# Leaving out TensorE's fifteen idle products of the identity at the start of a routed two-layer kernel

## The reference, cut to what matters

```
w   = weights[subjects]                       # 8 adapters of 32x32, one for each sample
z   = einsum('bct,bcd->bdt', x, w)            # tokens of a sample are mixed
logits = z @ Wg + bg                          # 4 experts
top 2 of 4, softmax, then for each expert the 1024 best tokens:
    out[sel] += gelu(tok @ W1[i]) @ W2[i] * p
x = x + out
gate, up, down with low-rank adapters by sample, silu(gate) * up, then a 256x256 product:
x = x + (h @ (w * scale).T + bias)
```

## Time and profile before

| | |
|---|---|
| median of three runs | 585.85 us (585.65 to 586.32) |
| profiled execution, its own time | 585.41 us |
| its span, first to last instruction | 583.6 us |
| PE busy | 567.9 us, 97% |
| PE on the chain that ended last | 93% |
| DVE on that chain | 5% |
| the idle products (line 1488) on that chain | 3.35 + 0.85 + 0.64 us |

### The profile page before, as it was taken

One profiled execution on the slowest core, in us unless ns is written; L12 is line 12 of the kernel. 1 busy time (PEld: TensorE's weight loads), 2 busy tenths in 40 slices (PEclk: granted clock), 3 DMA queues, 4 the chain that ended last, 5 costly groups with the idle time before them and its releaser, 6 DMA issues.

```text
span 583.6 us, 10462 instructions
## 1 busy us (share of the span) xinstructions
PE 567.9 (97%) x3629; PEld 475.9 (82%) x3629; DVE 371.4 (64%) x904; ACT 242.6 (42%) x548; POOL 138.6 (24%) x121
## 2 busy tenths in 40 slices
PE   7888999999999999999999999999999999999996
PEld 5766999999999999978878788788788788787885
DVE  7899667646775567675584474665655645755733
ACT  2664567748756655553312323224033223223110
POOL 2002311747346343664021030030030120100000
PEclk9999999999999999999999999999999999999999
DMA  8994677774285231434013032041041050220012
GB/s 326 343 361 177 200 244 222 196 182 72 47 259 145 47 41 20 128 62 136 1 46 102 8 109 47 0 133 22 0 137 16 4 140 9 76 49 4 13 25 37
DMA packets 64799, 61.06 MB, mean 105 GB/s; under 512 B 37456, under 2 KB 56656, under 8 KB 63472
## 3 DMA queue, kind: packets, MB, share of 16 engines
q1 hardware_dynamic: 53312, 37.97, 21.4%
q0 software_dynamic: 9264, 22.22, 15.6%
q10 hardware_dynamic: 2176, 0.26, 0.3%
HBM read 45.17 MB, written 19.47 MB: 111 GB/s over the span
## 4 chain that ended last, share of the span: by engine, by line
PE 93%; DVE 5%; DMA 1%; issue 0%; ACT 0%; POOL 0%; SPq 0%; DVEq 0%
PE bank L1455 26%; PE bank L1456 25%; PE bank L1457 25%; PE bank L1762 5%; PE bank L1720 3%; PE bank L1488 1%; PE bank L1471 1%; PE bank L1581 1%; DVE passed L887 1%; PE bank L1590 1%; PE bank L1712 1%; PE bank L1494 1%; PE bank L1729 1%; PE bank L1730 1%; PE bank L1539 1%; DVE passed_n L862 1%
## 5 line engine op out<-in xcount | busy, mean ns | idle before, releaser
L765 ACT ACTIVATE act<-bank 128x512 f32<-128x512 f32 x64 | 38.2, 598 | 182.9 <-PE bank L1762 182.9
L1411 DVE TENSOR_TENSOR prod<-bank,act 128x512 f32<-128x512 f32 x64 | 44.2, 691 | 97.5 <-PE bank L1762 97.1
L1267 DVE TENSOR_TENSOR hid_lo<-hf,hid_hi 128x512 fp32r<-128x512 f32 (+1 forms) x80 | 46.7, 585 | 52.5 <-ACT hf L686 52.1
L1455 PE MATMUL bank<-w_hi,hid_hi 128*128 128x256 f32 x256 | 71.7, 280 | 0.0
L1456 PE MATMUL bank<-w_lo,hid_hi 128*128 128x256 f32 x256 | 71.4, 279 | 0.0
L1457 PE MATMUL bank<-w_hi,hid_lo 128*128 128x256 f32 x256 | 71.3, 279 | 0.0
L683 ACT ACTIVATE hid_hi<-bank 128x512 fp32r<-128x512 f32 (+1 forms) x80 | 41.1, 514 | 65.0 <-PE bank L1457 63.3
L513 POOL DMA_INDIRECT x_rows<-y_sb,slot_row x32 | 52.6, 1644 | 43.1 <-ACT y_sb L653 27.3
L502 POOL DMA_INDIRECT xg<-flat_rows,slot_row x32 | 33.6, 1051 | 97.7 <-DVE slot_row L1112 49.3
L1455 PE MATMUL bank<-xs_hi,w_hi 128*128 128x512 f32 (+1 forms) x158 | 56.5, 357 | 0.0
L531 POOL DMA_INDIRECT b_pair<-b_rows,b_row x8 | 8.0, 1000 | 198.5 <-PE bank L1810 197.9
(11 more groups left out here) (326 smaller groups left out, 1269.8 us busy)
## 6 DMA issues: line engine op xcount, KB each, us to landing
w_raw<-in_L_ffn_W SPq DMA_DIRECT2D x8, 1024.0 KB, 6.9
flat_rows<-x_sb SPq DMA_DIRECT2D x8, 520.0 KB, 5.3
x_sb<-in_x SPq DMA_DIRECT2D x8, 512.0 KB, 8.6
x_rows<-in_x SPq DMA_DIRECT2D x4, 1024.0 KB, 8.1
outT<-out_sb SPq DMA_DIRECT2D x120, 32.0 KB
xT<-in_xT SPq DMA_DIRECT2D x3, 1024.0 KB, 7.4
xT<-in_xT SPq DMA_DIRECT2D x2, 512.0 KB, 10.6
wdT<-in_wdT SPq DMA_DIRECT2D x1, 1024.0 KB, 6.0
```

The lines of the kernel that those rows point to most:

```text
L765: act.activation(act1[h % 2][:, :], bank[h % 2][:, :], ACT.Silu).then_inc(silu1, 1)
L1267: dve.tensor_tensor(lo[:, n], hf[s % 2][:, n], hi[:, n].bitcast(f32), ALU.subtract).then_inc(hid0, 1)
L1411: dve.tensor_tensor(prod[par][h][:, :], bank[2 + h % 2][:, :], act1[h % 2][:, :], ALU.mult).then_inc(prod1, 1)
L1455: pe.matmul(out, lh, rh, start=start, stop=False, skip_group_check=True)
```

## The change

The function `idle_products` and its four calls are taken out. Nothing else is touched; the order on DVE and the DMA queue SP is the same, and on ACT and POOL only line numbers differ. Later lines of the kernel carry numbers that are lower by 5 (from `logits_of`), 8 (from the wait for `blocks_in`) and 9 (from the search).

```
-            def idle_products(n, into):
-
-                for _ in range(n):
-                    pe.matmul(into[:, 0:P], ident, ident, start=True, stop=True)
-
             def logits_of(half, adapters):
...
-            idle_products(7, bank[7])
             for i in range(7):
                 z_products(i)
                 if i in (2, 4, 6):
                     z_by_token(i // 2 - 1)
-                elif i in (1, 3):
-                    idle_products(2, bank[7])
             pe.wait_ge(blocks_in, 1)
...
             for n in range(ROWS_FIRST):
                 item(n)
-            idle_products(4, bank[4])
```

## The result

The changed kernel takes 587.86 us (median of 22 runs, 585.63 to 589.72), the kernel before in the same job 585.81 us (22 runs, 585.40 to 587.05). The ratio is 1.0026, 95% interval 1.0016 to 1.0035: a small loss, clear of no change; it stands just over the 0.2% that I had named, which lies inside its interval. (The ratio takes all runs into account and lies near that of the means, 1.0025; the medians' own is 1.0035.) The time lies in the predicted range (585.5 to 588.0), but not at 586.3, and the spread says more than the median: 8 of the changed kernel's runs lie between 585.6 and 587.2 us and 14 between 587.2 and 589.7. The mean granted clock of each of them parts them at the same place: 0.998 to 1.000 in the 8, 0.992 to 0.996 in the 14.

What follows compares the result with a forecast made beforehand. PE holds 93% of the chain and is full from 60 to 578 us, so the first 60 us set the end. Start +0.44 and search 0, added to the 585.85 us median, gave 586.3 us; range 585.5 to 588.0.

Steps and rivals of the forecast that it cites:

- no difference to be seen: Whole kernel: the forecast change lies below the 0.2% (1.2 us) that its times can tell; chance of same 0.66.
- a late rise (+0.44): Start: without idle products the clock rises at 13.33 us, so the turn at line 1482 starts at 14.72, not 14.28.
- rival 3: Search: the clock falls in the 1.5 us pause at 25.6 to 27.1 us; +1.5 us, 587.8 with part 1; chance 0.14.
- The path: PE's start delays line 908, then `slot_row`, POOL's gather and the end, one for one; gather at 54.5, not 54.1 us.
- rival 4: Start: the clock does not rise before the logits; +5 us, 591 us; chance 0.03.
- The data: Pieces of xT land at 6.98, 9.55, 12.17, 13.48 and 14.85 us; products start at about 7.03, 9.60 and 12.2 us.
- The rise: Start: PE's clock rises at 13.33 us, from first product at 7.03 plus 5.6 busy plus 0.70 pause; 12.6 to 14.5, chance 0.42.
- 5.6 us of PE busy: Start: PE busy time from its first product until the clock rises, taken from the one case in the trace.
- Rival 1: Start: the pause does not delay the rise, at 12.6 us or sooner; cost 0.0 to 0.15 us, 585.9 us; chance 0.18.
- rival 2: Start: the 0.70 us pause restarts the count, rise at 15.2 us; +1.18 us, 587.0, up to +1.7; chance 0.17.
- The four ahead of the search: Idle products behind the first 12 mixed rows: removal lengthens PE's pause to about 1.5 us, no clock fall, 0 us.

Runs made afterwards that it cites:

- e1: The changed kernel again, no edit; 589.84 us against 588.40 for the kernel before, ratio 1.0016.
- e4: Kernel before without the two pairs of idle products behind the calls on xT pieces 1 and 2; 588.79 us against 588.40, ratio 1.0003.
- e2: Kernel before without only the four idle products behind the first mixed rows; 588.13 us against 588.40, ratio 0.9996.
- e5: Kernel before plus five idle products at the search's end; 587.97 us against 588.11, ratio 1.0000.
- e10: Kernel before without the seven idle products ahead of the data, plus five at the search's end; 586.84 us against 585.93, ratio 1.0014.
- e9: Kernel before with one mixed row moved from the last search step to the one before it; 585.69 us against 585.93, ratio 1.0001.
- e11: Kernel before plus five idle products at the search's end and six products of zeros ahead of the identity wait; 586.23 us against 585.93, ratio 0.9999.
- e3: Kernel before without the eleven idle products of the start, last four kept; 589.82 us against 588.40, ratio 1.0023.
- e8: The changed kernel once more, in the job of e5 to e7; 590.57 us against 588.11 for the kernel before, ratio 1.0032.
- e12: The changed kernel a third time; 586.97 us against 586.38 for the kernel before, ratio 1.0018.
- e7: Kernel before without the eleven idle products of the start, four kept, five added at the search's end; 588.71 us against 588.11, ratio 1.0006.
- e6: Kernel before without all fifteen idle products, five added at the search's end; 588.74 us against 588.11, ratio 1.0009.

## Why the prediction was right or wrong

**The level and the direction.** The time lies in the range, but "no difference to be seen", the likeliest case, isn't what the runs show. The loss was to be the sum of a late rise (+0.44) and nothing; it is a late rise of 0 to 1.3 us and, in about half the runs, a fall of the clock on top. The forecast was +0.44 us, measured were +2.05 in median and +1.45 in mean; that this stayed in the range is owed to the upper end, which rival 3 had set with a fall at another place. The path was right: line 908 came 0.92 us later, the gather 0.88 us (54.96, forecast 54.5), and the last product of PE 0.98 us. In this profile the chain runs from `slot_row` over DVE's `w_lo` (line 1257) and not over the gather; both wait for `slot_row`. In rival 4 the sum compares the end of the turn (16.23 us) with the start of the one before (14.28); put right it is +4.6 us and not +5.

**The data (right, with a spread I left out).** Calls on pieces 1 and 2 started at 7.47 and 9.94 us in the changed kernel's first profile, for 7.03 and 9.60; in e1 they started at 6.99 and 9.46. The loads themselves vary by some 0.5 us, and without idle products in front PE follows them.

**The rise (right mechanism, size of the term off).** The profiles in a row give the rise and line 908's second addition:

| kernel | eleven at the start | clock up, us | line 908, us |
|---|---|---|---|
| before | in | 9.7 | 19.94 |
| e4 (seven of them) | in | 9.1 | 20.01 |
| e2 | in | 7.9 | 19.89 |
| e5 | in | 9.6 | 20.43 (data 0.50 late) |
| e10 (four of them) | in part | 10.9 | 20.41 |
| e9 | in | 8.5 | 20.24 (data 0.31 late) |
| e11 (and six of zeros) | in | 6.5 | 20.52 (piece 5 late) |
| e3 | out | 10.7 | 19.95 |
| e8 | out | 13.0 | 20.33 |
| e12 | out | 13.9 | 20.77 |
| changed | out | 13.9 | 20.86 (data 0.35 late) |
| e7 | out | 15.2 | 21.12 |
| e1 | out | 15.2 | 21.06 |
| e6 | out | 15.5 | 21.25 |

For the kernels without the eleven the working holds: I had 0 for a rise before 12.2 us (e3: +0.01), +0.44 for 13.33 (e8, 13.0: +0.39), +1.18 for 15.2 (e1 +1.12, e7 +1.18). What failed is the moment of the rise. The sum's 5.6 us of PE busy are the time from PE's first product at 4.04 us to the one rise on record, at about 9.65 us; that a pause adds to them was my estimate. No run shows 5.6 us as a fixed time: over these profiles the rise comes 3.5 to 8.4 us after PE's first product. It differs from run to run of one kernel, with 13.0, 13.9, 13.9 and 15.2 us in four profiles of the changed kernel. Rival 1 (e3, 10.7 us), the forecast (13.0 to 13.9) and rival 2 (15.2 to 15.5) all occur with the same program up to the logits. The start is then worth about 0.7 us, not 0.44: 0.74 in median (e7 against e5), and 0.66 as the difference of the mean of line 908 over the table's seven kernels with none of the eleven (20.76) and its five with at least seven of them and nothing added ahead (20.10).

**The four ahead of the search (right).** Cost 0: e2 0.9996, e6 equals e7. The pause of 1.45 us never showed a fall in a profile (changed, e1, e2, e6, e8, e12).

**Rival 3, the fall (right that there is one, wrong in place, and about right in price).** I had it behind the pause at 27 us, deciding the search, +1.5 us. It came at 49.3 us (e1) and 48.2 us (e3), where it hits the folds, +1.68 us there and 1.5 at the gather, and in e10 at 21.1 us. It lasted 3.4 us each time, and not 5.6 us of PE busy; PEclk is 1.00 in all fourteen profiles from 28 to 47 us, so none shows a slow step of the search as that rival had it. I had passed over the search's end although show its 0.75 us wait; I compared single waits and looked at the longest, and the clock had not fallen there in the one execution I had.

**How the median comes out.** In the jobs, 50 of 138 runs of the kernel before lie more than 1.2 us above their job's fastest. The mean granted clock says more than such a mark. It leaves out the time before the first rise (the changed kernel's profile, up at 13.9 us, has 0.999) and counts what is slow behind it: e1 and e3, with a fall, have 0.997. (So does e8's profile, whose only low stretch is the last 3.1 us, behind PE's last product; one run at 0.997 is no proof.) In the jobs of e9 to e12, 20 of the 46 runs of the kernel before have 0.997 or less. All 20 lie 1.0 us or more above their job's fastest, and 24 of the other 26 less than 0.7 us. So the kernel before has falls too, and it is not the change that brings them in. The clocks of the jobs of e1 to e8 don't part the runs so cleanly.

Of the changed kernel's 58 runs, 32 lie more than 2 us above before's fastest, the group that e1's profile with its fall belongs to. Where a third of the runs have a fall it leaves the median alone, where half have it it moves it. That would make the medians differ by 2.05, 1.44, 2.46 and 0.59 us in four jobs, when the ratios (1.0026, 1.0016, 1.0032, 1.0018) say 0.9 to 1.9 us. In the first job the difference in mean is 1.45 us. There 14 of 22 changed runs have a mean clock of 0.996 or less, and 6 of 22 of before's lie more than 1.0 us above the fastest (their clocks are not on record). If these are the falls, the estimate is 0.7 for the start and 0.36 x 1.7 = 0.6 for the falls, 1.3 in all. Four of the 14 have 0.993 or 0.992, by estimate 8 us and more at the 0.50 that the falls show (0.007 x 2 x 585), more than one fall of 3.4 us; no profile shows such a run.

**What stays open.** Whether the fall is truly more frequent without the eleven products isn't shown beyond the first job, and neither is why. On e12's chip 6 of 12 changed runs have a mean clock of 0.997 or less and 9 of 17 of before's, no difference. The later the clock rises, the later the search ends (e1: rise at 15.2 us, folds at 49.25; the kernel before: 9.7 and 48.15), but nothing shows that this brings a fall: e3 fell with an early rise, at 10.7 us. No profile of the kernel before shows its own fall, so the place of its falls is inferred from e1 and e3. And e9 says that idle time near the end isn't the measure of it.

## What to carry to other kernels

Products that do nothing are worth placing where an engine would wait for its first data anyway: here eleven of them are worth about 0.7 us at the start, because more of the slow time passes before the real work (the clock is up at 7.9 to 9.7 us in the five kernels with at least seven of them and nothing added ahead, at 10.7 to 15.5 in those with none). Where they outlast the wait they cost: in e10 the first pair put call 2 off by nearly 0.6 us. Where the clock changes at moments that the kernel doesn't set (here 13.0 to 15.2 us in one kernel), one profile shows one case of several: work the cost out for the whole range of moments, and look for every thin place, above all for one that stands just ahead of a stretch in which PE is full (here the search's end: with it covered none of 22 runs is over 589.84 us, without the cover seven of twelve in the same job). Look at the runs' spread before the median; two groups 1.5 us apart are two cases, not noise.

## What the runs showed of the hardware

- The granted clock fell to 0.50 for 3.4 us and came back in all three profiles with a fall (e1 at 49.3, e3 at 48.2, e10 at 21.1 us), each time with PE fully busy in between; it cost 1.7 us of PE time each (16 products of the folds 5.33 us for 3.65, twelve mixed rows 7.13 for 5.45). Of that 1.5 us reached the gather in e3 (against e4), 0.86 in e10 (against e5).
- Products of zeros seem to count towards the rise of the clock (e11, one profile: up at 6.5 us, with zeros from 1.12 us and the identity only from 4.16, 2.3 us before the rise; elsewhere the rise came 3.5 us or more after PE's first product).
- The moment of the rise, read from the durations, differs from run to run of one kernel: 13.0, 13.9, 13.9 and 15.2 us in four profiles of the changed one. PEclk reads 1.00 on both sides of it.
- The same waits of about 0.75, 0.53 and 0.68 us stand ahead of the folds in the kernel before, the changed one, e2, e4, e8 and e12, where no profile shows a fall, and in e1 and e3, which show one. In e9 the clock stayed up behind a wait of 1.05 us; in e10 it fell behind products with 64 columns, with PE shown busy for 2.43 us of the 2.72 just ahead. The share of time in which PE shows as busy is no sure sign of what the clock will do.
- Single runs can be far out: 636.4 us (e3, mean clock 0.851) and 692.3 us (e11, 0.770).
